# Degree term and output bias as bf16 products, own rows formed again by ScalarE, in the last walk of a four-layer graph kernel

## The reference

```python
h = jnp.maximum(_layernorm(x), 0.0)
x = x + layer(h, src, dst, ...)
```

```python
edge_inputs = concat([hidden[src], hidden[dst], edge_weight[:, None]], axis=1)
messages    = gelu(edge_inputs @ We1 + be1) @ We2 + be2
aggregated  = segment_sum(messages, dst)
u           = gelu(concat([hidden, aggregated], axis=1) @ Wu1 + bu1)
x           = x + _layernorm(hidden + (u @ Wu2 + bu2), gamma, beta)
```

## Time and profile before

| | us |
|---|---|
| median of 3 runs | 5151.64 |
| lowest, highest | 5151.11, 5152.08 |
| profiled execution, first to last instruction | 6457.2 |

### The profile page before, as it was taken

The page is one execution under the profiler, slowest core; times in us unless marked ns, Lnnn a source line. Parts: engine busy times, 40 slices in busy tenths (PEclk is TensorE's granted clock), DMA queues, the critical chain, the costliest instruction groups (busy, mean ns, idle before and its releaser), DMA issues. The chain is left out here.

```text
span 6457.2 us, 132161 instructions
## 1 busy us (share of the span) xinstructions
PE 4407.5 (68%) x23072; PEld 3228.9 (50%) x23073; DVE 3589.5 (56%) x12501; ACT 3052.6 (47%) x6864; POOL 3067.8 (48%) x3248
## 2 busy tenths in 40 slices
PE   7755555677657877577758999777771566666557
PEld 2333333566656655444436777566661444444345
DVE  9865555444436655466645665466661445455446
ACT  7533333444435555455545665355550334344335
POOL 0154445455545553545535555355545545554541
PEclk9877787777778998899989999899995767777778
DMA  0022222444434444466656787567762444444444
GB/s 18 10 62 66 66 67 72 128 153 154 146 110 149 152 141 135 158 211 215 215 170 214 241 250 242 169 227 231 235 226 86 133 127 141 131 140 133 130 130 140
DMA packets 613683, 956.80 MB, mean 148 GB/s; under 512 B 100096, under 2 KB 255888, under 8 KB 613584
## 3 DMA queue, kind: packets, MB, share of 16 engines
q1 hardware_dynamic: 494848, 746.65, 34.7%
q0 software_dynamic: 100672, 181.64, 11.8%
q10 hardware_dynamic: 18064, 27.47, 1.2%
HBM read 517.00 MB, written 438.38 MB: 148 GB/s over the span
## 5 line engine op out<-in xcount | busy, mean ns | idle before, releaser
L1045 PE MATMUL banks<-M,OH 128*128 x7840 | 1323.0, 319 | 654.8 <-issue 597.2
L588 POOL DMA_INDIRECT M<-table_a,six x1176 | 1117.8, 950 | 903.2 <-PE banks L1045 357.4
L1045 PEld LDWEIGHTS banks<-M,OH 128*128 128x128 f32 x7840 | 1148.7, 215 | 758.3 <-issue 739.2
L681 ACT ACTIVATE AG<-banks x1176 | 635.0, 591 | 1240.0 <-remote 954.3
L588 POOL DMA_INDIRECT M<-table_b,six x784 | 767.6, 979 | 627.0 <-PE banks L1042 208.5
L578 POOL DMA_INDIRECT edges_by_block<-pack,pos_i x392 | 376.5, 961 | 679.7 <-DVE pos_i L1325 558.7
L588 POOL DMA_INDIRECT M<-table_pairs,six x392 | 393.2, 1003 | 572.7 <-DVE ES L1581 451.3
L1441 DVE TENSOR_TENSOR OH<-banks,dstrel 128x1024 f32<-128x1024 f32 x392 | 478.3, 1221 | 221.7 <-remote 190.6
L681 ACT ACTIVATE HT<-banks 128x512 f32<-128x512 f32 x588 | 348.4, 593 | 513.2 <-remote 416.4
L699 ACT ACTIVATE HO<-H,BI,SC 128x128 f32 (+1 forms) x1176 | 485.3, 485 | 133.8 <-issue 73.4
L681 ACT ACTIVATE T<-banks 128x512 f32<-128x512 f32 (+1 forms) x686 | 355.0, 532 | 312.6 <-remote 124.3
(11 more groups left out here) (319 smaller groups left out, 8716.4 us busy)
## 6 DMA issues: line engine op xcount, KB each, us to landing
XZ<-state SPq DMA_DIRECT2D x490, 256.0 KB
table_a<-T SPq DMA_DIRECT2D x294, 256.0 KB
state<-T SPq DMA_DIRECT2D x294, 256.0 KB
state<-H SPq DMA_DIRECT2D x196, 256.0 KB
own_products<-T SPq DMA_DIRECT2D x98, 512.0 KB
table_pairs<-T SPq DMA_DIRECT2D x98, 512.0 KB
M<-messages SPq DMA_DIRECT2D x98, 512.0 KB
XZ<-in_x SPq DMA_DIRECT2D x194, 256.0 KB
```

The lines of the kernel that those rows point to most:

```text
L588: nc.gpsimd.indirect_dma_start(out=M[:, slot, :], out_offset=None, in_=table, in_offset=bass.IndirectOffsetOnAxis(ap=idx, axis=0)).then_in ...
L681: return nc.scalar.activation(dst_, src_, ACT.Copy)
L1045: last = mm(banks[:, ds(sums_at[k], P)], OH[:, b * US + k, :], source[:, ds(rows_at[k], P)], start=False, stop=False, skip_group_check=True)
```

## The change

In the last walk and in what it needs:

1. The degree product. The degrees are split into two bf16 parts (`dgh`, both exact for a whole number of this size), stored in DRAM as six rows (`deg_rows`: the high part three times, the low part three times). `cm` is split into three bf16 parts, laid out on six partitions (`cm6`). One bf16 product over six partitions takes the place of the float32 product over one.
2. The output bias. `bu2` is split as the bias of layer 1 is (`bu3`), and one bf16 product of `ones3` and `bu3`, broadcast over the four blocks, starts bank `ps[6 + b]`. `updated` no longer adds `bu2bc`.
3. The own rows. The four products with the identity are gone. ScalarE's new `own6`, at lag 11, forms `hidden` again from `x` into `HO`: four Relu activations with scale `nsr` and offset `ndr`. For this, walk 4 writes scale and offset of all groups to `nsr` and `ndr` (free by then) and not to `SC` and `BI`. `updated` adds `HO` to the bank, into `SX`.
4. The late load of `x` has four buffers (`rows_of`) and lag 10 in place of 12; ScalarE waits for it, and VectorE's `final` no longer does.

```diff
-            sp.wait_ge(s_dgc, 1)
-            sp.dma_start(deg_row.rearrange("(k c) p -> c k p", k=Q4), q(dgT[:, :])).then_inc(s_dr, 16)
-
             sp.wait_ge(s_rgc, 1)
             sp.dma_start(rdr_row.rearrange("(k c) p -> c k p", k=Q4), q(rgT[:, :])).then_inc(s_rst, 16)
+            sp.wait_ge(s_dgs, 1)
+            for r in range(6):
+                sp.dma_start(deg_rows[r].rearrange("(k c) p -> c k p", k=Q4), q(dgh[:, r // 3, :])).then_inc(s_dr, 16)
...
             def late6(i, b):
                 g = 2 * i + b
-                need(sp, s_fin, g - 1)
+                need(sp, s_fin, g - 3)
                 stand(sp)
-                sp.dma_start(XB[:, b, :], states[5][g]).then_inc(late[b], 16)
+                sp.dma_start(rows_of(i, b), states[5][g]).then_inc(late[b], 16)
...
-                sp.dma_start(RB[b], deg_row.rearrange("(g j) p -> g (j p)", j=Q4)[ds(g, 1), :]).then_inc(in_[b], 16)
+                sp.dma_start(RB[b], deg_rows.rearrange("r (g j) p -> g r (j p)", j=Q4)[g]).then_inc(in_[b], 16)
...
-            staggered(sp, [(LEADE + 3, load6), (0, store_edges), (5, load_edges), (LEADE + 5, late6), (LEADE + 7, store6)])
+            staggered(sp, [(LEADE + 3, load6), (0, store_edges), (5, load_edges), (LEADE + 3, late6), (LEADE + 7, store6)])
...
+                        elif d == 5:
+                            last = nc.scalar.activation(q(HO[:, b, :])[:, j, :], cell, ACT.Relu, bias=ndr[:, ds(g * Q4 + j, 1)], scale=nsr[:, ds(g * Q4 + j, 1)])
...
+            def own6(i, b):
+                g = 2 * i + b
+                act.wait_ge(late[b], turns(6, "late", i) + 16)
+                stand(act)
+                need(act, s_var, g + (at(6, "var") - 1))
+                stand(act)
+                for j in range(Q4):
+                    last = nc.scalar.activation(q(HO[:, b, :])[:, j, :], q(rows_of(i, b))[:, j, :], ACT.Relu, bias=ndr[:, ds(g * Q4 + j, 1)], scale=nsr[:, ds(g * Q4 + j, 1)])
+                last.then_inc(s_h5, 1)
+
...
-            staggered(act, [(1, messages), (LEADE + 5, hidden6), (LEADE + 2, copied6), (LEADE, sums(5)), (LEADE + 6, deviations(6, (s_fin, 0))), (LEADE + 3, turned(6))])
+            staggered(act, [(1, messages), (LEADE + 5, hidden6), (LEADE + 2, copied6), (LEADE, sums(5)), (LEADE + 6, deviations(6, (s_fin, 0))), (LEADE + 3, turned(6)), (LEADE + 4, own6)])
...
-                for j in range(Q4):
-                    mm(q(ps[6 + b])[:, j, :], q(H[:, b, 0, :])[:, j, :], ident[:, :], start=(j == 0), stop=False, skip_group_check=True)
+                mm(q(ps[6 + b]), ones3[:, :], bu3[:, :].rearrange("p (o d) -> p o d", o=1).broadcast_to([3 * 32, Q4, P]), start=True, stop=False, skip_group_check=True)
                 mm(ps[5], wu1[:, 0, :], H[:, b, 0, :], start=True, stop=False)
                 mm(ps[5], wm[:, :], HT[:, b, :], start=False, stop=False)
-                mm(ps[5], cm[:, :], RB[b], start=False, stop=True).then_inc(s_mma, 1)
+                mm(ps[5], cm6[:, :], RB[b], start=False, stop=True).then_inc(s_mma, 1)
...
-            link(v.tensor_copy(lb_rest[:, :], lbbc[:, :]))
+            for row3, whole_row in ((lb3, lbbc), (bu3, bu2bc)):
+                v.memset(row3[:, :], 0.0)
+                link(v.tensor_copy(lb_rest[:, :], whole_row[:, :]))
+                for k in range(3):
+                    link(v.tensor_copy(lb_part[:, k, :], lb_rest[:, :]))
...
+            link(v.tensor_copy(cmf[:, :], ps[7][0:6, P:2 * P]))
             for k in range(3):
...
+            link(v.tensor_copy(dgh[:, 0, :], dgT[:, :]))
+            v.tensor_tensor(dgh[:, 1, :], dgT[:, :], dgh[:, 0, :], ALU.subtract).then_inc(s_dgs, 1)
...
+                    if d == 5:
+                        stand(dve)
+                        marks["roots"] = chain.mark(v.reciprocal(nsr[:, ds(g * Q4, Q4)], SD[:, b, :]))
+                        return
...
             def updated(i, b):
                 g = 2 * i + b
                 dve.wait_ge(s_mm, g + (at(6, "mm") + 1))
-                link(v.tensor_tensor(q(Z[:, b, :]), q(ps[6 + b]), four(bu2bc), ALU.add))
-                spread(6, b, Z[:, b, :]).then_inc(s_var, 1)
+                dve.wait_ge(s_h5, g + 1)
+                link(v.tensor_tensor(SX[:, b, :], ps[6 + b], HO[:, b, :], ALU.add))
+                spread(6, b, SX[:, b, :]).then_inc(s_var, 1)
```

More of the change, by code:

```diff
@@ L218, in program @@
         dT = tmp("dT", [BC, 2, W4]); blkrep = tmp("blkrep", [BC, Q4, P]); nblk = tmp("nblk", [BC, Q4, P])
+        bu2bc = tmp("bu2bc", [P, P]); be2x = tmp("be2x", [P, 6]); cmf = tmp("cmf", [6, P]); cm_part = tmp("cm_part", [6, 3, P], BF16); third = tmp("third", [6, 3])
+        dgh = tmp("dgh", [BC, 2, W4], BF16)
         dgT = tmp("dgT", [BC, W4]); rgT = tmp("rgT", [BC, W4])
@@ L881, in _ @@
             mm(ps[7][:, 0:P], we2T[:, :], wu1[:, 1, :], start=True, stop=True)
-            mm(ps[7][0:1, P:2 * P], be2col[:, :], wu1[:, 1, :], start=True, stop=True).then_inc(s_wt, 1)
+            mm(ps[7][0:6, P:2 * P], be2x[:, :], wu1[:, 1, :], start=True, stop=True).then_inc(s_wt, 1)
             for k in (0, 1, 4):
@@ L1159, in _ @@
             dve.wait_ge(s_wt, 1)
+            v.tensor_copy(be2x[:, :], be2col[:, :].broadcast_to([P, 6]))
             v.tensor_copy(wlT[:, 0, :], ps[6][:, P:2 * P])
@@ L1164, in _ @@
             v.tensor_copy(wm[:, :], ps[7][:, 0:P])
-            v.tensor_copy(cm[:, :], ps[7][0:1, P:2 * P])
-            v.memset(lb3[:, :], 0.0)
             v.memset(ones3[:, :], 1.0)
-            link(v.tensor_copy(lb_rest[:, :], lbbc[:, :]))
+            for row3, whole_row in ((lb3, lbbc), (bu3, bu2bc)):
[3 more added lines that the diff above has]
+                    link(v.tensor_copy(lb_part[:, k, :], lb_rest[:, :]))
+                    v.tensor_copy(row3[k * 32:k * 32 + 1, :], lb_part[k * 32:k * 32 + 1, k, :])
+                    if k < 2:
+                        link(v.tensor_tensor(lb_rest[:, :], lb_rest[:, :], lb_part[:, k, :], ALU.subtract))
+            link(v.tensor_copy(cmf[:, :], ps[7][0:6, P:2 * P]))
             for k in range(3):
-                link(v.tensor_copy(lb_part[:, k, :], lb_rest[:, :]))
-                v.tensor_copy(lb3[k * 32:k * 32 + 1, :], lb_part[k * 32:k * 32 + 1, k, :])
+                link(v.tensor_scalar(third[:, k:k + 1], part_f[0:6, :], float(k), None, ALU.is_equal))
+                link(v.scalar_tensor_tensor(third[:, k:k + 1], part_f[0:6, :], float(k + 3), third[:, k:k + 1], ALU.is_equal, ALU.add))
+                link(v.tensor_copy(cm_part[:, k, :], cmf[:, :]))
                 if k < 2:
-                    link(v.tensor_tensor(lb_rest[:, :], lb_rest[:, :], lb_part[:, k, :], ALU.subtract))
+                    link(v.tensor_tensor(cmf[:, :], cmf[:, :], cm_part[:, k, :], ALU.subtract))
+            link(v.tensor_scalar(cm6[:, :], cm_part[:, 0, :], third[:, 0:1], None, ALU.mult))
+            for k in range(1, 3):
+                link(v.scalar_tensor_tensor(cm6[:, :], cm_part[:, k, :], third[:, k:k + 1], cm6[:, :], ALU.mult, ALU.add))
             link(v.tensor_copy(lane[:, :], iota_f[:, 0:P]))
@@ L1487, in offsets @@
                     chain.after(marks["roots"])
+                    if d == 5:
+                        g = 2 * i + b
+                        stand(dve)
+                        v.scalar_tensor_tensor(ndr[:, ds(g * Q4, Q4)], MV[:, b, :, 0], -1.0, nsr[:, ds(g * Q4, Q4)], ALU.mult, ALU.mult).then_inc(s_pre, 1)
+                        return
                     v.scalar_tensor_tensor(BI[:, b, :], MV[:, b, :, 0], -1.0, SC[:, b, :], ALU.mult, ALU.mult).then_inc(s_pre, 1)
@@ L1592, in final @@
                 v.reciprocal(SC[:, b, :], SD[:, b, :])
-                dve.wait_ge(late[b], turns(6, "late", i) + 16)
                 for j in range(Q4):
-                    v.tensor_tensor(q(XB[:, b, :])[:, j, :], q(XB[:, b, :])[:, j, :], bet[:, :], ALU.add)
+                    v.tensor_tensor(q(rows_of(i, b))[:, j, :], q(rows_of(i, b))[:, j, :], bet[:, :], ALU.add)
                 need(dve, st[b], turns(6, "st", i))
```

24 lines of the change are left out of this document (12 added, 12 removed).

## The result

| | us |
|---|---|
| kernel before, median of 4 runs beside it | 5151.38 |
| changed kernel, median of 4 runs | 5226.4 (5219.47 to 5232.7) |
| ratio | 1.0148, 95% interval 1.0134 to 1.0163 |

The changed kernel is 1.5% slower: 75 us, where I had forecast 5150 with a range of 5100 to 5180. The time lies outside the range.

What follows compares the result with a forecast made beforehand. POOL's gathers were taken to bound the last walk's middle and TensorE its end. Terms 5 + 1 + 4 - 5 - 6 = -1 us gave about 5150 us from 5151.6, range 5100 to 5180.

Steps and rivals of the forecast that it cites:

- The term put at nothing: Last walk: late load asked for two groups earlier, ScalarE waiting in own6; 0, or some us per group without cover.
- The burden of the profile: Whole kernel: crawling stretches taken mostly for a burden of the profiled execution, 6457.2 us against a median of 5151.64.
- POOL's pace in the middle: Middle of the last walk: POOL's eight gathers set the pace, 9.95 us a group, 975 us for 98 groups.
- TensorE's 1.5 us: Last walk: identity and float32 degree products go, two bf16 products come; -1.5 us a group, leaving 5.7.
- ScalarE's 1.65 us: Last walk: own6 adds four activations, 1.65 us for four as in walk 4; ScalarE from 6.4 to 8.0 us a group.
- The middle at -5 us: Middle of the last walk: POOL covers the changes on TensorE and ScalarE; -5 us over 85 groups.
- Rival (1): Middle of the last walk: TensorE's chain sets the pace; 150 us faster fully, 75 half, 20 weakly; chances 0.12 and 0.15.
- The end at -6 us: Last fourteen steps of the last walk: +1 us in eight where ScalarE takes over, -7 in six; -6 us.
- Ahead of the histogram and the ranking: VectorE's preparation: bias splitting and small operations +5 us before the histogram, two passes +1 us before the ranking.
- Walk 4 at +4 us: Walk 4: scale and offset written at computed addresses, one more register instruction each on VectorE; +4 us, between 0 and 11.
- Rival (3): Whole kernel: small costs come in full and the end gains nothing; +21 us, 5172 us; chance 0.12.
- rival (2): Middle of the last walk: TensorE's clock stays low, deciding below 0.57; +130 us, or half, +65; chance 0.07 together.

Runs made afterwards that it cites:

- identity kept: Changed kernel with the identity products back, own6 gone and the late load as before; bf16 products and preparation kept: 5149.8 us, 1.0001 of the kernel before.
- the load first: Changed kernel with the late load first in SyncE's step and one step later: 5312.62 us, 1.0324 of the kernel before; 0.9874 on a slow chip.

## Why the prediction was wrong, point by point

**The step that failed** is in the part on VectorE and the late load: "it is only asked for two groups earlier, and a whole step lies between, so I cost it at nothing; if that cover were gone it would be a landing of some us per group". No step lies between. I compared lag 10 on SyncE with lag 11 on ScalarE as if their steps were the same. They are not: ScalarE's `messages` has lag 1 and SyncE's `store_edges`, which waits for it, lag 0. So SyncE's step n-1 runs with ScalarE's step n, and the late load of SyncE's step n-1, behind that store, is the one `own6` waits for in ScalarE's step n. The order showed both lists; I read each for itself. I also asked who waits behind `own6` (the next messages, the next `hidden6`) without asking whom they release, which closes the ring. Its price could have been summed from links: gelu to store 0.85, store to load of messages 1.8, to the late load 0.8, landing and start of `own6` 5.2, `own6` 1.65, table load 1.3, about 11.6 us over POOL's 10.4. The words named the fallback, but it was no rival and had no chance; the range ended 46 us short of the result. The term put at nothing measured 62 to 65 us in the two profiles: 48.5 and 50 in the last walk's gathers, 14 and 15 behind the last one.

**The burden of the profile.** Wrong in its cause, as the run of the kernel before showed: it is the chip. The use I made of it was sound all the same: single durations taken from close-packed stretches are the same on both kinds (a gather 0.94 us, the sum out of the banks 0.69).

**POOL's pace in the middle.** Right as the bound, too small in size. 9.95 us a group came from the walk's first gathers; further on some of the eight take 1.05 to 1.13 us in place of 0.94, a group takes 10.4 to 10.5 us, and 98 take 1028, not 975.

**TensorE's 1.5 us.** Right. With `own6` later, at the end of the walk at the full clock:

```profile
5101.68 0.39 PE L1106 MATMUL banks<-bu,ones 96*128 96x512 bf16 x1 [1.16 <-DVE MV L1207]
5101.91 1.02 PE L1107 MATMUL banks<-H,wu 128*128 128x512 f32 x2
5102.77 1.02 PE L1108 MATMUL banks<-HT,wm 128*128 128x512 f32 x2
5103.72 0.38 PE L1109 MATMUL banks<-w,cm 6*128 6x512 bf16 x1
5104.04 1.16 PE L1115 MATMUL banks<-wu,H 128*128 128x128 f32 x8
```

The four parts take 2.36 us from start to start, and took 3.79: 1.43 less. From the start of each bf16 product to the next instruction are 0.23 and 0.32 us; I had 0.22 for each.

**ScalarE's 1.65 us** and no third table load: right to the hundredth, 1.65 us for four.

**The middle at -5 us**: in the versions without the ring it is -1.4 us (own6 later) and -0.2 (identity kept) for the gathers of the whole walk, and TensorE's shorter step gave nothing back. Rival (1), TensorE as the pace, is out: in the versions without the ring TensorE waits more than 220 of 900 us for VectorE's statistics, and POOL for nothing but "issue" to speak of.

**The end at -6 us**: -3.7 us with own6 later, and ScalarE did take over there, in steps of 7.12 us where I had said 7.3 (before 7.23). VectorE's `updated` in that version:

```profile
5085.26 0.69 DVE L1622 TENSOR_TENSOR SX<-banks,HO 128x512 f32<-128x512 f32 x1 [0.79 <-ACT HO L872]
5092.38 0.69 DVE L1622 TENSOR_TENSOR SX<-banks,HO 128x512 f32<-128x512 f32 x1 [0.79 <-ACT HO L872]
```

With the identity kept, where ScalarE has no `own6`, the steps are 6.68 us and the end is 8.0 us shorter than before. In the changed kernel the ring goes on past the last gather:

```profile
5128.41 0.69 DVE L1622 TENSOR_TENSOR SX<-banks,HO 128x512 f32<-128x512 f32 x1 [6.13 <-PE banks L1115]
5139.02 0.69 DVE L1622 TENSOR_TENSOR SX<-banks,HO 128x512 f32<-128x512 f32 x1 [4.28 <-PE banks L1115]
...
5158.74 0.69 DVE L1622 TENSOR_TENSOR SX<-banks,HO 128x512 f32<-128x512 f32 x1 [0.78 <-PE banks L1115]
5165.85 0.69 DVE L1622 TENSOR_TENSOR SX<-banks,HO 128x512 f32<-128x512 f32 x1 [0.79 <-PE banks L1115]
```

Steps of 10.6 to 12.5 us up to 5139, then two of 6.2 and 6.4, then 7.1: so the end became 14 to 15 us longer.

**Ahead of the histogram and the ranking**: I had +5 and +1. VectorE makes `lane`, the last piece ahead of the histogram, at 36.88 us before and here at

```profile
42.89 0.23 DVE L1198 COPY lane<-iota_f 128x128 f32<-128x128 f32 x1
```

6.0 us later, and the scatters begin 6.8 us later (7 to 9 in the profiles of all the changed kernels). Right to within 1 to 3 us. **Walk 4 at +4 us** can't be told from what walk 4 does from profile to profile (535 to 552 us). Rival (3) had the preparation about right (8.3 us) and the end wrong, which is 4 and 8 us shorter without the ring; its 5172 us didn't come.

**The clock.** The granted clock in the middle fell from 0.92 to 0.82 in the changed kernel, and to 0.81 with the ring broken; with the identity kept it is 0.88. So it goes with TensorE's missing work, not with the ring, and it cost nothing that can be measured (0.9996), since POOL sets the pace there. That is the mechanism of rival (2), but far from the 0.57 from which it would decide. The Trainium skill, page "TensorE: Matmul & The Clock Gate", section "HAM oscillation — how this bites in real kernels", says that gaps between bursts let the clock fall; the trace agrees in direction, 0.92 to 0.81 with less work between the same waits.

The sum without the ring would have held: 5147.45 us with own6 later, 5149.8 with the identity kept, against 5150. Neither beats the kernel before: what they save at the end, 4 and 8 us, the preparation takes back (the scatters begin 8 us later in both profiles).

## What to carry to other kernels

Lags of two engines can only be compared through a semaphore that ties their steps: before a load is called early enough, find the instruction that stands ahead of it in its queue, what that one waits for, and whether the reader of the load is upstream of it. If it is, sum the ring link by link, landing included, and hold it against the step of the engine that sets the pace. A ring shows in a profile as one engine waiting nearly the same time in every step, and it passes on most of any work that is added inside it (65 of 81 us here, 14 outside). One step more of lag for the reader opened it here, and so, but for 12 us, did a place for the load ahead of the store; one step more of lag for the load made it longer.

## What the runs showed of the hardware that I had not expected

- The same program takes 5150 us on some chips and 6390 on another, a quarter more, with single instructions of the same length and gaps named "issue" between them. An edit that costs 3.2% on the first kind (the load first) gained 1.3% on the second.
- The late load, 256 KB, landed 3.8 to 6.3 us after its issue, median 4.5, from 4100 to 5000 us, with 183 GB/s in all over the stretch; its issue at 4703.74 came 3.5 us after the start of the gelu that released SyncE's list ahead of it.
- A gather (most take 0.94 us) lasts longer where it meets `onehots`, VectorE's operation of 1.2 us over 128x1024. In the nine profiles from chips of the first kind, 250 gathers of the last walk take 1.5 us or more. Every one begins 0.05 to 0.54 us behind the start of an `onehots` and ends 2.01 to 2.08 us behind it.
- A bf16 product of 512 columns is recorded at 0.39 us with 96 rows and at 0.38 with 6: fewer rows did not make it shorter. The next instruction starts 0.23 us behind the one and 0.32 behind the other, and it isn't the same instruction.
